# Attention and FFN layer in one kernel: pairs in groups of two, an order of its own for each engine, shared banks for scores and transposes

## The reference

```python
x = x + layernorm(attention(layernorm(x)))   # 16 heads of 64, softmax over 256 keys, output projection + b_O
x = x + layernorm(ffn(layernorm(x)))
# ffn: base = x @ W.T; gate = softmax(x @ gate_w.T) over 8; t = x @ lora_U (8 x 16)
#      out = base + (1/16) * (gate * t) @ lora_V
```

## Time and profile before

| | |
|---|---|
| median of 3 runs | 1333.15 us (1332.89 to 1333.64) |
| the profiled execution, first to last instruction (span) | 1331.8 us |
| TensorE matmuls busy | 1239.1 us, 93% |
| VectorE busy | 1165.5 us, 88% |
| ScalarE busy | 1036.3 us, 78% |
| GpSimd busy | 710.5 us, 53% |
| mean granted TensorE clock | 0.993 |
| chain that ended last | PE 56%, DVE 36%, issue 6% |

### The profile page before, as it was taken

The page is one execution under the profiler, slowest core; times in us unless marked ns, Lnnn a source line. Parts: engine busy times, 40 slices in busy tenths (PEclk is TensorE's granted clock), DMA queues, the critical chain, the costliest instruction groups (busy, mean ns, idle before and its releaser), DMA issues.

```text
span 1331.8 us, 32877 instructions
## 1 busy us (share of the span) xinstructions
PE 1239.1 (93%) x10496; PEld 969.3 (73%) x10496; DVE 1165.5 (88%) x3305; ACT 1036.3 (78%) x3465; POOL 710.5 (53%) x805
## 2 busy tenths in 40 slices
PE   6999999999999999999999999999999999999994
PEld 4777777777777777777777777777777777777773
DVE  6898988898888999888989888998889898889883
ACT  6887787878878777778877778788787778788782
POOL 3455555545555555555555555545555555555552
PEclk9999999999999999999999999999999999999997
DMA  6000000000000000000000000000000000000000
GB/s 196 1 6 1 4 4 4 4 4 0 4 4 4 4 0 4 4 4 4 4 0 4 4 4 4 4 0 4 4 4 4 0 4 4 4 4 4 0 5 9
DMA packets 9924, 10.96 MB, mean 8 GB/s; under 512 B 816, under 2 KB 9392, under 8 KB 9904
## 3 DMA queue, kind: packets, MB, share of 16 engines
q1 hardware_dynamic: 9904, 10.70, 2.4%
HBM read 6.50 MB, written 4.19 MB: 8 GB/s over the span
## 4 chain that ended last, share of the span: by engine, by line
PE 56%; DVE 36%; issue 6%; ACT 1%; POOL 1%; DVEq 0%; DMA 0%; POOLq 0%; ACTq 0%
PE probs_t_ps L335 10%; PE o_ps L361 10%; PE scores L322 9%; PE extra_ps L381 8%; PE qk_ps L274 4%; DVE q_lo L618 4%; DVE neg_max L681 4%; DVE k_lo L621 4%; DVE y L643 3%; DVE probs_t L704 3%; PE qk_ps L276 3%; PE qk_ps L275 3%; DVE gate L744 3%; DVE x1n L643 2%; DVE stats L629 2%
## 5 line engine op out<-in xcount | busy, mean ns | idle before, releaser
L861 POOL TENSOR_TENSOR probs<-probs,inv_sum 128x512 f32<-128x512 f32 x512 | 529.9, 1040 | 414.5 <-DVE inv_sum L688 414.5
L519 ACT ACTIVATE probs<-scores,neg_max 128x256 f32<-128x256 f32 x1024 | 480.9, 483 | 152.7 <-DVE neg_max L681 152.7
L681 DVE TENSOR_REDUCE neg_max<-scores 128x2 f32<-128x512 f32 x512 | 348.2, 680 | 28.3 <-PE scores L322 28.0
L361 PE MATMUL o_ps<-probs_t,v_sb 128*64 128x256 f32 x2048 | 277.5, 391 | 27.5 <-DVE o_lo L695 26.0
L335 PE MATMUL probs_t_ps<-ident,probs 128*128 128x128 f32 x2048 | 276.4, 273 | 2.7 <-ACT probs_t L529 1.3
L335 PEld LDWEIGHTS probs_t_ps<-ident,probs 128*128 128x128 f32 x2048 | 232.5, 141 | 8.7 <-POOL probs L861 2.1
L704 DVE COPY probs_t<-probs_t_ps 128x512 f32<-128x512 f32 x256 | 175.3, 685 | 58.7 <-PE probs_t_ps L335 58.5
L519 ACT ACTIVATION_READ_ACCUMULATOR probs<-scores,neg_max 128x1 f32 x1024 | 217.9, 213 | 0.0
L361 PEld LDWEIGHTS o_ps<-probs_t,v_sb 128*64 128x64 f32 x2048 | 129.7, 136 | 110.1 <-issue 72.6
L832 POOL TENSOR_TENSOR rstd<-var_eps,neg_half 128x2 f32<-128x2 f32 x128 | 88.6, 692 | 189.1 <-DVE var_eps L638 189.1
L322 PE MATMUL scores<-k_hi,q_hi 64*128 64x256 f32 x1024 | 171.4, 331 | 1.1 <-ACT probs L519 1.1
(11 more groups left out here) (92 smaller groups left out, 2379.9 us busy)
## 6 DMA issues: line engine op xcount, KB each, us to landing
out<-x_all SPq DMA_DIRECT2D x32, 128.0 KB, 1.7
x_all<-in_x SPq DMA_DIRECT2D x1, 3840.0 KB, 17.4
stage_v<-in_w_v SPq DMA_DIRECT2D x1, 512.0 KB, 4.1
stage_o<-in_w_o SPq DMA_DIRECT2D x1, 512.0 KB, 6.7
stage_q<-in_w_q SPq DMA_DIRECT2D x1, 384.0 KB, 4.5
stage_k<-in_w_k SPq DMA_DIRECT2D x1, 384.0 KB, 5.8
x_all<-in_x SPq DMA_DIRECT2D x2, 128.0 KB, 3.0
ffn<-in_ffn_w SPq DMA_DIRECT2D x1, 196.0 KB, 6.7
```

The source lines that it names most:

```text
L361: last = nc.tensor.matmul(o_ps[head_rows(h), 0:T], v_sb[:, s, pair * P + h * DH:pair * P + (h + 1) * DH], probs_t[par][h][:, s, :], start= ...
L519: last = nc.scalar.activation(probs[par][h][:, j, :], scores_ps[h][par][:, j * T:(j + 1) * T], ACT.Exp, bias=neg_max[par][h][:, j:j + 1], ...
L681: nc.vector.tensor_reduce(neg_max[par][h][:, :], scores_ps[h][par][:, :].rearrange("p (j s) -> p j s", j=NT), AX.X, ALU.max, negate=True). ...
L861: nc.gpsimd.tensor_tensor(probs[par][h][:, :, :], probs[par][h][:, :, :], inv_sum[par][h][:, :].unsqueeze(2).to_broadcast([P, NT, T]), ALU ...
```

## The change

- PSUM: four banks st_ps[pair parity][head] hold first a head's scores and then its transposed probabilities; qk_ps becomes two banks; o_ps holds the two pairs of a group side by side. scores of pair p+2 wait for both copies of pair p.
- q, k, probs and probs_t, with their small tiles, have four buffers.
- o_hi and o_lo are made for a group of two pairs at a time, with one semaphore step a group. probs_v of a group's second pair has no wait for the bank.
- Both heads' scores are signalled together at the end of the six (now one scores_ready).
- The loop has one body a turn, and each engine has its own lag: run(engine, lag, body) unrolls lag + 1 bodies in front and lag behind; TensorE, ScalarE and GpSimd reach back two batches, VectorE three.
- More waits are written out (x1_transposed, z_projected, out_ready, y_transposed and others), where a buffer's last reader was before covered by order.
- Every engine has one order for a body. The four, shortened: a prime is batch i-1, two primes i-2, three i-3; the digit is the pair (or quarter of v, or group of two pairs for o and op), the letter after it the head (a = 0, b = 1).

The core of the diff:

```diff
+N_QK, N_PROBS, N_PROBS_T = 4, 4, 4
...
-        scores_ps = [[bank("scores0")] * 2, [bank("scores10"), bank("scores11")]]
-        probs_t_ps = [bank(f"probs_t_ps{h}") for h in range(2)]
-        qk_ps = bank("qk_ps")
+        st_ps = [[bank(f"st_ps{n}{h}") for h in range(2)] for n in range(2)]
+        qk_ps = [bank(f"qk_ps{n}") for n in range(2)]
         o_ps = bank("o_ps")
         extra_ps = bank("extra_ps")
...
+        def run(engine, lag, body):
+
+            for i in range(lag + 1):
+                body(i)
+            with engine.Fori(0, B - 1 - lag) as step:
+                body(step + (lag + 1))
+            for i in range(B, B + lag):
+                body(i)
...
+            def scores(b, p, free0, free1):
+                pe.wait_ge(qk_lo_ready, PAIRS * b + p + 1)
+                after(pe, *free0)
+                after(pe, *free1)
+                n = p % N_QK
+                terms = ((q_hi[n], k_hi[n]), (q_hi[n], k_lo[n]), (q_lo[n], k_hi[n]))
+                for j in range(NT):
+                    for t, (q, k) in enumerate(terms):
+                        for h in range(2):
+                            last = nc.tensor.matmul(st_ps[p % 2][h][:, j * T:(j + 1) * T],
+                                                    tile(q, j)[head_rows(h), :], k[head_rows(h), :],
+                                                    start=(t == 0), stop=(t == 2))
+                last.then_inc(scores_ready, 1)
+
+            def transpose_probs(b, p, h, free):
+                pe.wait_ge(probs_ready[h], PAIRS * b + p + 1)
+                after(pe, *free)
+                for j in range(NT):
+                    for s in range(NT):
+                        last = nc.tensor.transpose(
+                            st_ps[p % 2][h][:, s * T + j * P:s * T + (j + 1) * P],
+                            probs[p % N_PROBS][h][:, j, s * P:(s + 1) * P], ident[:, :])
+                last.then_inc(probs_transposed[h], 1)
+
+            def probs_v(b, p, free=None):
+                for h in range(2):
+                    pe.wait_ge(probs_t_copied[h], PAIRS * b + p + 1)
+                if p % (PAIRS // 2) == 0:
+                    for j in range(NT):
+                        pe.wait_ge(v_copied[p // (PAIRS // 2) * 2 + j], b + 1)
+                if free is not None:
+                    after(pe, *free)
+                cols = slice(p % 2 * T, (p % 2 + 1) * T)
+                for s in range(NT):
+                    for h in range(2):
+                        last = nc.tensor.matmul(
+                            o_ps[head_rows(h), cols],
+                            v_sb[:, s, p * P + h * DH:p * P + (h + 1) * DH],
+                            probs_t[p % N_PROBS_T][h][:, s, :], start=(s == 0), stop=(s == NT - 1))
+                last.then_inc(o_projected, 1)
+
...
+            def exponentials(b, p, h):
+                act.wait_ge(max_ready[h], PAIRS * b + p + 1)
+                after(act, probs_transposed[h], PAIRS * b + p + 1 - N_PROBS)
+                n = p % N_PROBS
+                for j in range(NT):
+                    last = nc.scalar.activation(probs[n][h][:, j, :], st_ps[p % 2][h][:, j * T:(j + 1) * T],
+                                                ACT.Exp, bias=neg_max[n][h][:, j:j + 1],
+                                                accum_out=row_sum[n][h][:, j:j + 1])
+                last.then_inc(exp_ready[h], 1)
+
+            def copy_probs_t(b, p):
+                act.wait_ge(probs_transposed[0], PAIRS * b + p + 1)
+                after(act, o_projected, PAIRS * b + p + 1 - N_PROBS_T)
+                nc.scalar.copy(probs_t[p % N_PROBS_T][0][:, :, :].rearrange("p s q -> p (s q)"),
+                               st_ps[p % 2][0][:, :]).then_inc(probs_t_copied[0], 1)
+
+            def attention_hi(b, group):
+                act.wait_ge(o_projected, PAIRS * b + 2 * group + 2)
+                for n, pair in enumerate((2 * group, 2 * group + 1)):
+                    last = nc.scalar.activation(o_hi[:, pair, :], o_ps[:, n * T:(n + 1) * T], ACT.Identity,
+                                                bias=bias[:, B_V + pair:B_V + pair + 1])
+                last.then_inc(o_hi_ready, 1)
+
...
+            def row_max(b, p, h):
+                dve.wait_ge(scores_ready, PAIRS * b + p + 1)
+                nc.vector.tensor_reduce(neg_max[p % N_PROBS][h][:, :],
+                                        st_ps[p % 2][h][:, :].rearrange("p (j s) -> p j s", j=NT),
+                                        AX.X, ALU.max, negate=True).then_inc(max_ready[h], 1)
```

More of the change, by code:

```diff
@@ L59, in after, with live, latest, first @@
         engine.wait_ge(sem, count)
+def live(i, lag):
+    return not isinstance(i, int) or 0 <= i - lag < B
+def latest(i, *uses):
+    for lag, sem, count in uses:
+        if live(i, lag):
+            return sem, count
+    return uses[0][1], 0
+def first(b):
+    return isinstance(b, int) and b == 0
 def transformer_layer(nc, x, w_q, w_k, w_v, w_o, biases, ffn_w, out):
@@ L277, in project_qk, with project_v @@
                 last.then_inc(qk_projected, 1)
-            def transpose_tiles(dst, src):
-                for j in range(NT):
-                    last = nc.tensor.transpose(tile(dst, j), tile(src, j), ident[:, :])
-                return last
-            def project_v(dst, quarter):
+            def project_v(b, quarter, free):
+                if first(b) and quarter == 0:
+                    pe.wait_ge(w_lo_ready["v"], 1)
+                if quarter == 0:
+                    pe.wait_ge(xt_lo_ready, b + 1)
+                after(pe, *free)
@@ new lines, in output_projection @@
+            def output_projection(b, group, free=None):
+                if first(b) and group == 0:
+                    pe.wait_ge(w_lo_ready["o"], 1)
+                if free is not None:
+                    after(pe, *free)
+                pe.wait_ge(o_lo_ready, GROUPS * b + group + 1)
+                for pair in (2 * group, 2 * group + 1):
+                    cols = pair_cols(pair)
+                    for n, (w, o) in enumerate(((w_hi, o_hi), (w_hi, o_lo), (w_lo, o_hi))):
+                        last = nc.tensor.matmul(extra_ps[:, 0:T], w["o"][:, cols], o[:, pair, :],
+                                                start=(pair == 0 and n == 0),
+                                                stop=(pair == PAIRS - 1 and n == 2))
+                if group == GROUPS - 1:
+                    last.then_inc(yt_projected, 1)
@@ new lines, in transpose_y, with transpose_x1n, project_tg @@
+            def transpose_y(b, free):
+                after(pe, *free)
+                pe.wait_ge(yt_ready, b + 1)
+                transpose_tiles(extra_ps, yt).then_inc(y_transposed, 1)
+            def transpose_x1n(b, free):
+                after(pe, *free)
+                pe.wait_ge(x1n_ready, b + 1)
+                transpose_tiles(extra_ps, x1n).then_inc(x1_transposed, 1)
+            def project_tg(b, free):
+                if first(b):
+                    pe.wait_ge(ffn_scaled, 1)
+                after(pe, *free)
+                pe.wait_ge(x1t_ready, b + 1)
+                for j in range(NT):
+                    last = nc.tensor.matmul(extra_ps[:, j * TG:(j + 1) * TG], tile(x1t, j),
+                                            ffn[:, F_TG:F_TG + TG], start=True, stop=True)
+                last.then_inc(tg_projected, 1)
@@ L611, in _ @@
+            run(act, 2, body)
         @block.vector
@@ new lines, in stats_x1, with norm_x1, copy_x1t @@
+            def stats_x1(b):
+                dve.wait_ge(x1_ready, b + 1)
+                ln_stats(LN_X1, x1, b + 1)
+            def norm_x1(b):
+                dve.wait_ge(rstd_ready[LN_X1], b + 1)
+                after(dve, x1_transposed, b)
+                ln_apply(LN_X1, x1n, x1).then_inc(x1n_ready, 1)
+            def copy_x1t(b):
+                dve.wait_ge(x1_transposed, b + 1)
+                after(dve, z_projected, b)
+                nc.vector.tensor_copy(x1t[:, :], extra_ps[:, 0:T]).then_inc(x1t_ready, 1)
@@ L821, in _ @@
+            run(dve, 3, body)
         @block.gpsimd
```

973 lines of the change are left out of this document (490 added, 483 removed).

## The result

| | before | after |
|---|---|---|
| median of the runs, us (lowest to highest) | 1333.13 (1332.89 to 1333.64) | 1255.51 (1254.08 to 1255.66) |
| ratio, 95% interval | 1 | 0.9416 (0.9402 to 0.9429) |
| span of the profiled execution, us | 1331.8 | 1253.8 |
| a loop body in the middle, us | 40.42 to 40.58 | 37.80 |
| TensorE idle in it, us | 1.9 to 2.1 | 0.59 |

What follows compares the result with a forecast made beforehand. TensorE was taken to bound the kernel. Body 0 40.0, body 1 36.9, 30 bodies of 38.7, then 5.3 and 37.1 gave 1280.3; with 1.35 outside the span 1281.6, said 1282 us, range 1264 to 1325.

Steps and rivals of the forecast that it cites:

- the three stalls: TensorE's waits for o_lo, u and xt_lo, once a batch each, together 2.0 us; said to go.
- P: Time of one loop body after the change: 37.7 work, 0.85 waits, 0.1 loop turns, taken as 38.7 us.
- Entering probs_v from scores: On TensorE, four times a batch after; no row, 0.17 us taken each, nothing or twice that possible.
- the 0.28 a stretch: TensorE's price of a probs_v stretch, 0.17 entering and 0.11 leaving; three fewer stretches save 0.8 us a batch.
- (a): TensorE's scores 5 wait for VectorE's copy of pair 3, behind stats_x1; 0.1 to 0.2 us late.
- (b): Next body's scores 6, at 38.75, wait for VectorE's copy of pair 4, which ends at 38.9.
- (c): TensorE's probs_v 2, at 35.6, waits for o_lo of group 0, ready at 35.6 to 35.7.
- the five with little in hand: Copies of pairs 1 and 5, scales of 2, 4 and 5: 0.1 to 0.2 us in hand, 0.4 counted.
- Loop turns: One body a turn on TensorE, 29 turns for 15; 0.08 us more a batch, taken as 0.1.
- that rival: Port lock: VectorE and GpSimd shut each other out, VectorE becomes the bound; P = 39.6, 1309 us, chance 0.21.
- Bank turnaround: Rival: scores wait for copies out of shared banks; at a turnaround of 10.3, P = 41.2, 1357 us; chance 0.16.
- air: Room in the shared banks' turns between pairs; in the placement only the turn from pair 4 to 6 had none.

Runs made afterwards that it cites:

- split_matched: split_pv with VectorE's reciprocals of pair 0 head 0 and pair 3 head 1 moved ahead of the row_max they stood behind; 1287.79 us.
- split_by_qk: Kernel after with probs_v groups 4+5 and 0+1 each pulled apart by a projection on TensorE; 1267.54 us.
- next1: Kernel after with scores 5 before pair 4's head-0 transposes, VectorE's pair 3 copy before stats_x1, pair 1 copy between pair 2's row_max; 1277.26 us.
- before_grouped: Kernel before with only probs_v, o_hi and o_lo grouped by two pairs and four probs_t buffers, one query-key bank kept; 1409.82 us.
- u_early: Kernel after with u's transpose three groups earlier on TensorE, ahead of v's second quarter; 1307.99 us.
- split_pv: Kernel after with probs_v groups 6+7 and 0+1 pulled apart on TensorE by scores 1 and scores 4; 1305.62 us.

## Why the prediction was wrong in size

The direction, the bound and the mechanism held: TensorE bounds both kernels, the three stalls went, and nothing took their place in full. The time missed the range at its low end. By the prediction's own sum, term by term:

| term | predicted | measured | on the time |
|---|---|---|---|
| body 0, from 0 | 40.0 | 43.66 | +3.7 |
| body 1 | 36.9 | 37.27 | +0.4 |
| a body of the loop, x 30 | 38.7 | 37.79 | -27.3 |
| rest behind it | 5.3 + 37.1 | 39.2 | -3.2 |
| outside the span, of the median | 1.35 | 1.7 | +0.4 |

The failed term is P, 38.7 said and 37.8 measured, and in it two numbers of nearly one size, work and waits.

*Work, 37.7 said, 37.3 measured.* The step was "Entering probs_v from scores (four times a batch after) has no row; it may cost nothing or twice the 0.17". It costs nothing: scores take 0.91 before probs_v as before anything else, so the 4 x 0.17 that I put in don't exist. Against that, the price of a change of form is smaller than the 0.28 a stretch that I took from the earlier trace rows. Its 0.11 "for leaving probs_v" is no price of probs_v: in the kernel before the first step of scores is 0.22 behind a v quarter (656.00 to 656.22) and 0.23 behind probs_v (660.39 to 660.62), so where scores follow, a stretch less saves nothing at its end.

```profile
656.22 0.28 PE L322 MATMUL scores<-k_lo,q_hi 64*128 64x256 f32 x2
```

By run, split_matched gives 0.17 for a stretch more behind scores, split_by_qk 0.26 behind a projection. What matters is the kind of matmul ahead: transposes ahead of probs_v step 0.53 for 0.36, a projection 0.90 for 0.79, scores no more than ever. The sum of TensorE's savings by kind is 1.16 (0.45 in probs_v, 0.36 in the transposes, 0.22 in the lone transposes and tg, 0.10 in scores), for the 0.84 predicted.

*Waits, 0.85 said, 0.48 measured.* Three places were placed late: (a) the copy of pair 3 before scores 5, (b) the copy of pair 4 before scores 6, (c) o_lo before probs_v 2. In the trace none of them waits, (b) by the 0.19 us shown above, and (a) only because the transposes of pair 4 ahead of scores 5 had waited 0.32 already: in next1, with scores 5 in front of them, it waits 0.18 for that copy. The placement put scores 6 at 38.75 and the copy's end at 38.9; relative to the transpose of xn they are at 38.17 and 37.98. I had x1n at 0.95, which took 0.81, and counted row_max and copies singly where pairs run on. Of the five with little in hand, the scale of pair 4 waits 0.32 and the copy of pair 1 0.16. So the 0.4 for the five was about right, at 0.48, and the 0.45 for the three was not there.

*Loop turns, 0.1 said, nothing measured.* Two bodies a turn changed 1255.51 to 1255.49. The earlier trace rows had the right sign: the queue that carries instructions moved 11 packets after as well, and 16 with two bodies a turn, in the same time. The Trainium skill, "Runtime: NRT & Kernel Launch", section "Instruction fetch mechanics", says that a branch out of the buffered window forces a DMA fetch; neither the packets nor this pair of runs shows a price for it here.

*VectorE.* Gate's two at 0.36, y's at 1.51 and the string of 9.2 us came as predicted. Busy time fell to 35.0 rather than 36, and x1n's two were 0.81, in the last 0.47 us of a scale. The lock of two engines is thus in this order too, on y in full, but it does not bound the kernel, and next1 shows that two moved items bring it there. The price of that rival was also mis-added: 28.8 + 10.4 closes at 39.2, not at P = 39.6. The Trainium skill, "SBUF — State Buffer", section "Who interferes with whom", describes such a lock of VectorE and GpSimd; the trace agrees with x1n's two at 0.60 with GpSimd idle, 0.81 on the end of a scale, and 1.30 in next1, where they start 0.07 us behind the start of one.

*Bank turnaround.* It didn't decide, and its price was real: split_matched delays two scores by 1.0 us and pays 0.69 of idle time a body for it, 0.58 of it in scores that wait for a copy. The "air" that the placement saw is smaller than 1.0 us.

*Buffers and banks.* Rightly nothing: fourfold probabilities. Wrongly argued: "Fourfold buffers, two query-key banks and the explicit waits ... cost nothing and bring nothing". Grouping puts two scores and two projections nearer to each other, and one bank then stalls TensorE three times a body (2.35 us). I looked at what the second bank adds, not at what the grouping takes from the first. It made no error in the sum, since the change has both. The kernel after with one query-key bank was not tried: it would need another order, and would not be the same experiment.

*The ends.* Body 0 took 38.2 from the transpose of xn for the 35 said; TensorE's clock was at 0.91 in it and it was idle for 8.8 us. From scores 7 of the last batch to the end took 35.0 us, not the 37.1: there the last group's o_hi and o_lo (1227.09 to 1228.84) lay beside z and its copy, for which the output projection waited until 1228.60 in any case, and beside its first pairs. The two nearly cancel.

The range was too narrow at its low end. I had said that entering probs_v may cost nothing (-0.7 a body) and that all hand-overs may be in time (-0.85), and then gave everything under 1267 no more than 0.03. Over 30 bodies they are worth 21 and 26 us, and about half of each came true.

## What to carry to other kernels

Where an engine runs a fixed list and is 95% busy, ask of each item that leaves its place what it had been hiding: in the kernel before, the single pair's probs_v between projections hid a bank's emptying, and grouping without a second bank lost 5.8%. In the queue of another engine, what needs a late input must stand behind what does not: two reciprocals that stood behind row_max cost 0.6 us a turn together. And when two unknown costs are each bounded by zero, the range must reach to where both are zero.

## What the runs showed of the hardware

A matmul's price depends on the form of its neighbour, and not symmetrically. A group of probs_v (tiles of 128 by 64) alone steps 1.01 to 1.02 us and two adjoined 1.88; scores (64 by 128) ahead of it step 0.91 as always; of those with 128 by 128, a projection ahead of it steps 0.90 for 0.79, transposes 0.53 for 0.36.

Short waits in a row can cost more than themselves: in before_grouped, after TensorE was busy 1.85 of 3.71 us, its granted clock stood at 0.50 for some 3 us, in 14 of 29 bodies, at 1.6 us each. The same stretch in the other 15 bodies left it at 1.00, so the waits don't settle it, and what else does stays open. Waits of 0.40 and 0.87 us a body, as in u_early, stood beside a mean clock of the whole run of 0.99.

The profile's idle time understates a wait behind a matmul, since it begins only where the row ahead ends: the transposes of pair 0 in split_pv last 0.66 us in their rows where the usual step is 0.4, and start 1.04 apart with 0.38 called idle. The step from start to start tells it.
